# Attention inside a fused attention and mixture-of-experts kernel: the values product of a group of heads in one block of four chunks, and the output projection dealt as three chunks, one, three, one

## What is computed

```python
def attention(q, ctx, Wc, bc):             # q = layernorm(x), keys = values = ctx
    # 16 heads of 64; 4 groups of 4 heads share one 64-wide key/value head
    probs = softmax(einsum('bghsd,bgtd->bghst', qh, kh) / 8)
    out = einsum('bghst,bgtd->bghsd', probs, vh)          # the values product
    return out.reshape(b, s, 1024) @ Wc.T + bc            # the output projection
x = x + attention(layernorm(x), ctx_512, Wc, bc)
# experts: softmax router over 32 experts, 8 per row, silu(x Wg) * (x Wu) @ Wd, weighted sum
x = x + experts(layernorm(x), ...)
```

## Time and profile before

| what | value |
|---|---|
| median of 3 runs | 9380.23 us |
| the profiled execution | 9384.3 us |
| its span (first to last instruction) | 9382.5 us |
| TensorE busy | 9131.8 us, 97% of the span |
| VectorE, ScalarE, GpSimd busy | 67%, 44%, 56% |
| mean granted TensorE clock | 0.99 |

### The profile page before, as it was taken

The page is one execution under the profiler, slowest core; times in us unless marked ns, Lnnn a source line. Parts: engine busy times, 40 slices in busy tenths (PEclk is TensorE's granted clock), DMA queues, the critical chain, the costliest instruction groups (busy, mean ns, idle before and its releaser), DMA issues.

```text
span 9382.5 us, 175724 instructions
## 1 busy us (share of the span) xinstructions
PE 9131.8 (97%) x47664; PEld 7354.4 (78%) x47665; DVE 6312.3 (67%) x9152; ACT 4150.8 (44%) x6947; POOL 5265.5 (56%) x4825
## 2 busy tenths in 40 slices
PE   8999999999959999999999999999999999999999
PEld 5666666666647888888888888888888888888888
DVE  5666666666646767777666677677777677766676
ACT  5666666666633433343333333333333333333333
POOL 2444444444446656666555666566666566656564
PEclk9999999999979999999999999999999999999999
DMA  2221212112114545555444455455555455544544
GB/s 97 57 59 59 62 55 64 58 55 64 54 61 106 119 106 118 116 128 129 109 108 110 111 132 117 106 115 114 116 115 128 104 125 114 115 107 111 127 113 83
DMA packets 787086, 926.19 MB, mean 99 GB/s; under 512 B 403473, under 2 KB 600081, under 8 KB 786578
## 3 DMA queue, kind: packets, MB, share of 16 engines
q0 software_dynamic: 209920, 604.72, 29.5%
q1 hardware_dynamic: 430866, 165.82, 7.2%
q10 hardware_dynamic: 145920, 151.01, 5.0%
HBM read 1076.32 MB, written 376.45 MB: 155 GB/s over the span
## 4 chain that ended last, share of the span: by engine, by line
PE 67%; issue 1%; DVE 1%; ACTq 1%; ACT 0%; POOL 0%; DMA 0%; DVEq 0%; SPq 0%; POOLq 0%
PE bank L1593 44%; PE bank L1616 23%; DVE xT_lo L1501 0%; ACTq L1395 0%; ACTq L1387 0%; POOL xg L1341 0%; ACT xT_hi L1408 0%; DVE rows_out L1531 0%; ACTq L1385 0%; DMA entry_in<-slot_table 0%; DVE gu_lo L1507 0%; DVE xT L1496 0%; DVE h_lo L1524 0%; DVE h L1519 0%; DMA xg<-xn_rows,gather_row 0%
## 5 line engine op out<-in xcount | busy, mean ns | idle before, releaser
L1341 POOL DMA_INDIRECT xg<-xn_rows,gather_row x2304 | 2954.7, 1282 | 1838.6 <-PE bank L1593 1353.7
L1593 PE MATMUL bank<-xT_hi,gu_hi 128*128 128x512 f32 (+2 forms) x6912 | 2558.2, 370 | 121.1 <-DVE xT_lo L1501 114.6
L1593 PE MATMUL bank<-xT_lo,gu_hi 128*128 128x512 f32 (+2 forms) x6912 | 2545.6, 368 | 0.0
L1593 PE MATMUL bank<-xT_hi,gu_lo 128*128 128x512 f32 (+2 forms) x6912 | 2545.3, 368 | 0.0
L1426 ACT ACTIVATE gated<-bank 128x512 f32<-128x512 f32 x432 | 258.6, 599 | 3028.0 <-PE bank L1593 3010.1
L1593 PEld LDWEIGHTS bank<-xT_hi,gu_hi 128*128 128x128 f32 x6912 | 1301.1, 188 | 305.1 <-issue 90.4
L1353 POOL DMA_INDIRECT out_rows<-rows_out,entry_now x576 | 1110.0, 1927 | 698.6 <-DVE rows_out L1531 412.8
L1593 PEld LDWEIGHTS bank<-xT_lo,gu_hi 128*128 128x128 f32 x6912 | 1301.5, 188 | 158.6
L1593 PEld LDWEIGHTS bank<-xT_hi,gu_lo 128*128 128x128 f32 x6912 | 1300.9, 188 | 158.5
L1496 DVE STREAM_TRANSPOSE xT<-xg 128x512 f32<-128x512 f32 x1152 | 1283.4, 1155 | 13.6 <-DMA xg<-xn_rows,gather_row 13.6
L1616 PE MATMUL bank<-d_hi,h_hi 128*128 128x512 f32 x3162 | 1244.8, 394 | 19.0 <-DVE h_lo L1524 8.7
(11 more groups left out here) (158 smaller groups left out, 12304.3 us busy)
## 6 DMA issues: line engine op xcount, KB each, us to landing
d_raw<-in_L_ffn_down_proj ACTq DMA_DIRECT2D x144, 1536.0 KB
gu_raw<-in_L_ffn_gate_proj ACTq DMA_DIRECT2D x145, 1024.0 KB
gu_raw<-in_L_ffn_up_proj ACTq DMA_DIRECT2D x145, 1024.0 KB
gu_raw<-in_L_ffn_gate_proj ACTq DMA_DIRECT2D x145, 512.0 KB
gu_raw<-in_L_ffn_up_proj ACTq DMA_DIRECT2D x145, 512.0 KB
xg<-xn_rows,gather_row POOLq DMA_INDIRECT x2304
x_t<-in_x SPq DMA_DIRECT2D x64, 512.0 KB, 4.7
inv_wide<-inverse_sums SPq DMA_DIRECT2D x512, 64.0 KB
```

What stands on the lines that cost most here:

```text
L1341: pool.indirect_dma_start(out=xg[:, m, :], out_offset=None, in_=quarter_rows, in_offset=bass.IndirectOffsetOnAxis(ap=gather_row[:, m:m + 1 ...
L1593: last = nc.tensor.matmul(bank[:, 0:cols], w[:, c, n, j * P:(j + 1) * P], v[:, c, 0:cols], start=(c == 0 and w is gu_hi and v is xT_hi), s ...
```

## The change

Three tables of steps change. The values product of a group stands in one block of four chunks at `h` % 4 = 1. The projection takes three chunks at `h` % 4 = 0 and one at `h` % 4 = 2. The normalisation of the last group of the tile before (`OUT_NORM`, group 3) moves from step 4 to step 2, and its low part from step 5 to step 3. All engines follow the same tables. The number of instructions that compute is the same.

```diff
-            OUT_NORM = {0: (1, 2), 4: (1, 3), 8: (0, 0), 12: (0, 1)}
+            OUT_NORM = {0: (1, 2), 2: (1, 3), 8: (0, 0), 12: (0, 1)}
             DVE_HEAD = 1
-            VALUE_CHUNKS = {1: (0, 1), 3: (2, 3)}
-
-            PROJECT = {h: (1, h // GROUP_HEADS // 2, h % 8, h % 8 + 2) for h in range(0, H, 2)}
+            VALUE_CHUNKS = {1: (0, 1, 2, 3)}
+
+            PROJECT = {0: (1, 0, 0, 3), 2: (1, 0, 3, 4), 4: (1, 0, 4, 7), 6: (1, 0, 7, 8),
+                       8: (1, 1, 0, 3), 10: (1, 1, 3, 4), 12: (1, 1, 4, 7), 14: (1, 1, 7, 8)}
```

## The result

The changed kernel takes 9361.4 us (median of 14 runs, 9355.42 to 9368.75) against 9379.65 of the kernel before, run beside it: 18 us less, ratio 0.9979 [0.9972, 0.9987]. Forecast were 55 us less, and 9296 to 9364 for the time. The time lies in that range, at its slow end, but the gain is a third of the one forecast. The profiled execution has a span of 9359.0 us.

The account below looks back on a forecast made before the run. PE, busy 97% of the span, was taken as the bound. Block edges gave 78 us, less 16 x (0.9 + 0.26) and 4 for small waits: 55 us, 9380 to 9325 us; own range 9310 to 9340, wider range 9296 to 9364.

Parts of the forecast that it names:

- Stretches without X ... become some 4.0 us: Scores block (S) to next S without router transposes (X), such as from step 15: some 4.0 us after the change.
- what is late next: Next S waits for both exponentials, 3.28 us after the last S; stretches of 4.0 to 4.45 leave 0.7 to 1.2 us cover.
- Edges of a values block: PE, values block between two probability transposes: joining the halves saves 0.305 us per group, 78 us gross (61 to 95).
- the sum: Whole program: 78 - 16 x (0.9 + 0.26) = 59 us, 4 off for small waits, so 55 us gained.
- Where a sequence ends: Sequence boundary: DVE sets the time; X and P end 0.8 us later, the tile reaches step 7 0.3 us later.
- The deal 3, 1, 3, 1: Projection blocks: takes nothing off PE, moves stretches between S blocks; step 1 + 0.17, step 3 - 0.47 us with the values block.
- The normalisation at step 2: DVE and ACT: maxima some 0.35 us later, 0.2 us cover left at X, cost zero.
- Rival C: DVE at step 2 waits for the inverse's late load, delaying S: at 3 us late 58 us slower, 9438; 4%.
- the 0.9 us per sequence: Loss at each sequence's start: such a tile reaches step 7 0.3 us later, an undisturbed one 0.6 earlier.
- The 0.26 us at step 13 of the last tile: Last tile of a sequence: PE waits at step 13 for ACT's query copy, behind a values copy; 0.26 us, an estimate.
- Rival D: PE's clock falls once a tile, slowing six projection matmuls and a scores block some 1.5 us: + 41 us, 9421; 2%.

Follow-up runs that it names:

- the early logits: The changed kernel with the copy of the router's logits moved to the end of step 6: 0.9924 of the kernel before (9322.2 us), again 0.9925 (9307.5 us).
- the even deal: Projection dealt two chunks at every even step, as in the kernel before; put back into the changed kernel with the logits' copy at step 6: 0.9980, 9373.3 us.
- the late copy: The kernel before with one unused DVE addition ahead of the logits' copy of step 7: 1.0013 of the kernel before, 9407.0 against 9393.9 us.
- the values block alone: The kernel before with only the values product in one block of four chunks, projection and normalisation unchanged: 0.9971 in the first series, 1.0038 in the third.

## Why the prediction was wrong

**The step that failed** is "Stretches without X ... become some 4.0 us", with "what is late next" behind it: I asked only for the exponentials as the next wait. For step 15 it was right (4.02 us). For step 7 P has a wait of its own, on the logits' copy, whose cover was the half values block that leaves. The wait measured 0.72 us in three tiles of a sequence and 1.3 in the first (5.33 us for 4.02), some 55 us; the early logits give 47 to 53 back. The prediction had this term at nothing. "What wait stands on the instruction that now comes sooner" was to be asked of each of the eight projection blocks, not of S alone. The line was in the code and the 0.55 us in the trace.

**Edges of a values block: right.** Two transposes in a row and then P take 0.84 us (forecast 0.49 + 0.36 = 0.85), sixteen values records 1.88 from first to next start (1.01 + 0.865). The seven other stretches of a regular tile came out within 0.03 us, and without the logits' wait a regular tile is 1.22 us shorter (39.15 for 40.37): 78 us in 64, as in the sum. The stage as a whole is then 61 to 67 us shorter and the program 72, where the sum had 59 and 4 off: the term for the sequences was too large, as told below under "Where a sequence ends".

**The deal 3, 1, 3, 1: half right.** It takes nothing off PE, but it is worth 0.7 us a tile as cover for the query copy, and more where a sequence begins. I had set it down as "moves the stretches", and had not priced the even deal. No run has the deal alone in the kernel before.

**The normalisation at step 2: right.** DVE came to it as forecast (919.74, 3.73 us after the S of 916.01), the maxima started at 922.04, 0.36 us later than minimal, and X did not wait in regular tiles. Rival C did not happen: the waits view has one wait for the inverse's DMA in 1000 us, of 0.2 us; before it has two, 0.4 in all.

**Where a sequence ends: half right.** The stretch of step 3 was to end 0.8 us later than before; it takes 5.69 us (median) for 4.92, and X waits for ScalarE there (6.1 us in 6 sequences), as the text says. But the S at its start was forecast at its old time, and came 0.7 us earlier: the stretches of step 15 and step 1 across the boundary fell from 5.73 and 6.05 us on average to 5.28 and 5.80. So such a tile reaches step 7 0.4 us earlier than before, not 0.3 later, and the 0.9 us per sequence was 0.2, some 11 us too much in the sum. The 0.26 us at step 13 of the last tile measured 0.2. From step 7 on the first tile pays the longer logits' wait: from the S of step 1 to the next tile's it takes 42.68 us, for 42.54 before.

**Rival D** was given as every tile or none; that a fall comes in each tile was my supposition, and no run shows it. It came true in a few: the granted clock falls from 1.00 to 0.50 behind step 6, where one chunk of projection now stands between the router and S, in 2 of some 60 tiles in one profile of the changed kernel and in 5 in the other. The kernel before fell to 0.50 twice in the stage, at 384.1 and 1879.2 us, both times at the start of a sequence, behind stops of 2.03 and 1.84 us. Windows of such a tile and of the 7 us ahead of it (the number before the DMA share is the granted clock), then PE's timeline:

```profile
1012.50:1015.90 3.40, 3.40 (x16) 2.55 (x15) 1.92 (x8) 1.41 (x5) 0.00 (x0) 0.50 0.14 39
1005.00:1012.00 7.00, 6.75 (x53) 4.97 (x53) 2.91 (x9) 4.35 (x9) 2.51 (x7) 1.00 0.08 21
```
```profile
1009.58 1.97 PE L875 MATMUL bank<-gate_sb,xn2T 128*128 128x32 f32 x16 [0.25 <-ACT xn2T L504]
1011.39 0.48 PE L853 MATMUL bank<-WcT_hi,oT_hi 128*128 128x512 f32 x1
...
1013.66 1.97 PE L811 MATMUL bank<-ident,probs 128*128 128x128 f32 x8
1015.28 0.77 PE L853 MATMUL bank<-WcT_hi,oT_hi 128*128 128x512 f32 x1
```

The eight transposes take 1.62 us to P in place of 0.84. A fall costs 0.8 us beside the logits' wait (5.58 for 4.74) and 1.6 without it (5.58 for 4.02): 2 to 4 us in the profiles of the changed kernel, 5 to 6 in those of the early logits on the second and third chip, 13 on the first (8 tiles).

In the seven profiles of kernels with the even deal no tile fell there (0 of some 60 in each). Two of these kernels have the values in one block, so the same transposes meet and the same router follows; the one with the early copy differs from the early logits by the deal alone. So that transposes meet isn't enough: falls at this step came only in kernels with one projection chunk (three matmuls) behind the router in place of two, and in each of their seven profiles, in 2 to 8 tiles. Whether the falls need the meeting transposes as well is open: no run has the new deal with the values in two blocks.

## What to carry to other kernels

When work is taken out between two instructions, every wait of the one that now comes sooner has lost its cover; list those waits from the code (buffer releases above all), and read for each in the trace how long ago it was met (here 0.55 us before the change, with 0.70 us of waiting after it). Two equal pieces moved about can be worth nothing on the bound engine and still be needed as cover (here one chunk of projection, 51 us in the whole program). Where queues are this regular, the distance between two recurring instructions, by position in the loop, shows a loss of 0.7 us a round at once, when the total shows only a missing gain.

## What the runs showed of the hardware

On the chip of the first series the kernel before took 9506.9 us, for 9379 to 9394 on the others. That kernel wasn't profiled there. The kernel before with the logits moved, which changes nothing there or elsewhere (1.000 and 0.9998), was, and its trace has a stop at step 13 in nearly every tile. PE and DVE of that trace, timeline:

```profile
976.35 0.53 PE L770 MATMUL bank<-ident_r,xq 128*128 128x128 f32 x4 [0.77 <-issue]
...
977.15 0.69 DVE L586 TENSOR_REDUCE neg_max<-bank 128x1 f32<-128x512 f32 x1 [3.98 <-remote]
```

The stretch of step 13 is some 6.3 us there. The same program on the third chip has no such stop; its stretch is 4.82 us, as in the first trace. On the first chip the stage is 69 us longer for it, and neither engine waits for anything that the profile shows ("issue" and "remote"). The cause is open. The packets of the profile's queue q8, "instruction", don't tell it: they last 1.16 us on average there and 1.05 in the first trace, but 1.15 in that of the late copy, which has no such stop. So no run shows that the chips differ in how they deliver instructions, as one expectation above has it. The kernel with the values block alone had no such stop (5.70 us on both chips), the early logits a small one (5.2 for 4.98). So on that chip edits were paid or charged for something that they don't contain: the values block alone won 0.3% there and lost 0.4% elsewhere. The experts stage was 52 to 68 us longer on it too: 6615 to 6634 us from its first matmul to the end in four kernels, for 6562 to 6567 in the same four on the third chip.
